# Attention and feed-forward block: subtraction in one pass, new places for transfers and tanh, six banks for the last group's scores

## The reference

```
x = x + attn(wkv(x, fside, fside, w, u, cond), w_qkv, w_o)
x = x + ffn(wkv(x, fside, fside, w2, u2, cond), w_gate, w_up, w_down)

# wkv(r, k, v): k = v = fside
ek = exp(min(k, 30)); ekv = ek * v            # running sums a = a*decay + ek, forward and backward
num = nf + nb - ekv + euk*v;  den = df + db - ek + euk      # euk = exp(min(u + k, 30))
out = sigmoid(r) * num / max(den, 1e-8) * (0.8 + 0.2*tf)

# attn: 16 heads of 32, causal
probs = softmax(mask(q @ k.T / sqrt(32)));  return (probs @ v) @ w_o.T

# ffn: inputs and weights rounded to blocks of 32 with a shared exponent
return q_act(silu(q_act(x) @ q_w(w_gate).T) * (q_act(x) @ q_w(w_up).T)) @ q_w(w_down).T
```

## Time and profile before

| | |
|---|---|
| median of 3 runs | 885.54 us (885.06 to 889.25) |
| profiled execution, its own time | 888.3 us |
| its span, first to last instruction | 886.6 us |
| mean granted TensorE clock | 0.949 of 2.4 GHz |
| TensorE busy | 753.3 us (85%) |
| VectorE busy | 755.0 us (85%) |
| ScalarE busy | 510.0 us (58%) |
| DMA issues `stacks<-rows`, SP and POOL | 128 each, 128 KB each |

### The profile page before, as it was taken

The page is one execution under the profiler, slowest core; times in us unless marked ns, Lnnn a source line. Parts: engine busy times, 40 slices in busy tenths (PEclk is TensorE's granted clock), DMA queues, the critical chain, the costliest instruction groups (busy, mean ns, idle before and its releaser), DMA issues.

```text
span 886.6 us, 10871 instructions
## 1 busy us (share of the span) xinstructions
PE 753.3 (85%) x3980; PEld 393.7 (44%) x4017; DVE 755.0 (85%) x1070; ACT 510.0 (58%) x754; POOL 74.8 (8%) x149
## 2 busy tenths in 40 slices
PE   4667659698789999988799999888999998989785
PEld 1222224345444444455444444454444444557674
DVE  4899999998998878989988798899897888743887
ACT  4966655368575474577763664867736636443440
POOL 1000001102000002111000021110000131200000
PEclk9786678899999999999999999999999999999998
DMA  9623311456100004754010037540100084500001
GB/s 335 253 88 107 106 60 40 98 124 167 48 25 24 1 12 124 191 141 116 13 36 1 13 76 221 155 119 13 36 1 12 13 221 129 125 1 1 1 1 48
DMA packets 31253, 73.08 MB, mean 82 GB/s; under 512 B 5856, under 2 KB 6880, under 8 KB 29408
## 3 DMA queue, kind: packets, MB, share of 16 engines
q1 hardware_dynamic: 19584, 46.67, 17.5%
q0 software_dynamic: 6144, 16.79, 8.1%
q10 hardware_dynamic: 5472, 8.92, 3.2%
HBM read 34.61 MB, written 4.19 MB: 44 GB/s over the span
## 4 chain that ended last, share of the span: by engine, by line
PE 40%; DVE 31%; issue 10%; ACT 8%; DMA 6%; SPq 3%; POOL 1%; ACTq 0%; DVEq 0%
PE bank L1591 9%; DMA stacks<-rows 5%; PE bank L1469 5%; PE bank L1458 4%; PE bank L1373 4%; DVE negmax L1068 4%; SPq L331 3%; PE bank L1440 3%; ACT region L575 3%; PE bank L1496 2%; PE bank L1381 2%; PE bank L1407 2%; DVE num L974 2%; PE bank L1387 2%; DVE fn L960 1%
## 5 line engine op out<-in xcount | busy, mean ns | idle before, releaser
L331 POOL DMA_DIRECT2D stacks<-rows x128 | 70.7, 560 | 696.7 <-DVE region L1114 347.1
L575 ACT ACTIVATE region<-bank 128x384 f32<-128x384 f32 (+1 forms) x192 | 95.5, 522 | 54.5 <-PE bank L1443 52.5
L1440 PE MATMUL bank<-stacks 128*128 128x512 f32 (+3 forms) x256 | 104.7, 415 | 25.0 <-ACT region L575 24.8
L1068 DVE TENSOR_REDUCE negmax<-bank 128x4 f32<-128x512 f32 (+2 forms) x96 | 98.5, 1035 | 27.6 <-PE bank L1414 14.7
L1381 PE MATMUL bank<-h,wqkv 128*128 128x512 f32 x256 | 115.5, 605 | 0.0
L1407 PE MATMUL bank<-stacks 128*128 128x128 f32 (+3 forms) x256 | 77.7, 398 | 12.8 <-DVE negmax L1068 6.6
L1381 PEld LDWEIGHTS bank<-h,wqkv 128*128 128x128 f32 x256 | 49.0, 194 | 58.0 <-issue 57.6
L1440 PEld LDWEIGHTS bank<-stacks 128*128 128x128 f32 x256 | 49.7, 194 | 54.5 <-ACT region L575 45.3
L1442 PE MATMUL bank<-maxrow,pick 128*128 128x384 bf16 (+3 forms) x236 | 72.5, 307 | 0.0
L1373 PE MATMUL bank<-wqkv,h 128*128 128x512 f32 x128 | 61.4, 624 | 4.7 <-DVE h L1008 4.7
L1643 PE MATMUL bank<-region,ident 128*128 128x512 f32 x64 | 49.5, 934 | 12.7 <-DVE identb L919 12.7
(11 more groups left out here) (196 smaller groups left out, 1526.0 us busy)
## 6 DMA issues: line engine op xcount, KB each, us to landing
stacks<-rows SPq DMA_DIRECT2D x128, 128.0 KB, 3.4
stacks<-rows POOLq DMA_DIRECT2D x128, 128.0 KB, 4.6
...
```

The source lines that it names most:

```text
L331: eng.dma_start(stacks[HD * r:HD * r + HD, at:at + 2, i, :].bitcast(F32), rows[mine, q:k + 1:k - q, :]).then_inc(stacked[s][i], 16)
L575: nc.scalar.activation(probs[:, i, P_AT[tiles[0]]:P_AT[tiles[0]] + columns], bank[4 + n % 2][:, 0:columns], ACT.Exp, scale=SCALE).then_inc ...
L1068: nc.vector.tensor_reduce(o, scored, AX_X, ALU.max, negate=True).then_inc(max_taken, 1)
L1440: nc.tensor.matmul(o, ks[s][:, i, P * t:P * t + P], qs[s][:, i, P * t:T], start=True, stop=False, skip_group_check=True)
```

## The change

It has nine parts; no matmul, exponential or scan is added or left out.

1. `less_ident` and the places 2 to 5 of `rows` (under the new name `rounded_rows`, the same memory) are of type fp32r, so that the subtraction has two rounded operands.
2. The next batch's group 0 transfers wait for the second rounding to eighths (`rounded_8`) and no longer for the second scaled quarter (`iq_ready`).
3. SP sends the load of x into `h` only when group 2's transfers have landed. The tanh stands behind `cap_exp(5)`, and its second table load behind `floored(4)`.
4. TensorE: group 1's subtraction of the next batch stands before the last quarter of the down projection. In turns 1 to 3 the projection of group 2 goes before the first scores, and that of the values before slots 4 and 5.
5. ScalarE: `late_high_parts` and both weighings of unit 2 stand before `copy_maxima(0)`.
6. VectorE: `backward(1, 1)` and `add_own(1)` stand before the residual at a turn's end; a new order of the turn's first steps for b > 0.
7. VectorE: a maximum is taken before `backward(4, 1)`, `backward(5, 0)`, `backward(5, 1)` and `forward(6, 0)`.
8. Last group: scores by key go round banks 4, 5, 0, 1, 2, 3; tile n waits for the exponential of tile n - 6, and tile 2 for all maxima.
9. ScalarE in the last group: the maxima's copy and one exponential before the weighings of unit 6; `cap_exp(7)` behind the ninth exponential.

The diff, without the longer lists of part 6 (shown as order below):

```diff
@@ -78,7 +78,7 @@
         identb = sb("identb", [P, P], BF16)
-        less_ident = sb("less_ident", [P, P], F32)
+        less_ident = sb("less_ident", [P, P], F32R)
         hide_kq = sb("hide_kq", [P, P], BF16)
@@ -110,8 +110,9 @@
         v_sb = sb("v_sb", [P, TT, C], F32)
+        rows_at = (nc.sbuf_base + 31) // 32 * 32
         rows = sb("rows", [P, 8, T], F32)
-        halves = rows[:, 2:6, :].bitcast(F32R)
+        rounded_rows = nc.alloc_sbuf_tensor_at("rounded_rows", [P, 4, T], F32R, offset=rows_at + 2 * T * 4)
         attn = [rows[:, n, :] for n in (0, 6, 1, 7)]
@@ -257,6 +258,10 @@
+        def key_bank(g, n):
+            return bank[(4, 5, 0, 1, 2, 3)[n % 6]] if g == GROUPS - 1 else bank[4 + n % 2]
         def qk_banks(g):
@@ -326,10 +331,11 @@
                 mine = slice(HD * i, HD * i + HD)
+                source, base = (rounded_rows.bitcast(F32), 2) if g < 2 else (rows, 0)
                 q_high, q_low, k_high, k_low = ((2, 3, 4, 5), (2, 3, 4, 5), (2, 0, 4, 6), (3, 1, 5, 7))[g]
...
                     eng.dma_start(stacks[HD * r:HD * r + HD, at:at + 2, i, :].bitcast(F32),
-                                  rows[mine, q:k + 1:k - q, :]).then_inc(stacked[s][i], 16)
+                                  source[mine, q - base:k - base + 1:k - q, :]).then_inc(stacked[s][i], 16)
@@ -364,10 +370,12 @@
                     sp.wait_ge(v_ready, b * TT + TT)
+                    for head in stacked[0]:
+                        sp.wait_ge(head, (b + 1) * (STACK_INC * GROUPS // 2))
                     sp.dma_start(h[:, :, :], x[b + 1]).then_inc(h_in, 16)
...
                 if more:
-                    sp.wait_ge(iq_ready, b * FC + 2)
+                    sp.wait_ge(rounded_8, b * FC + 2)
                     stack(sp, b + 1, 0, 0, 2)
@@ -423,7 +431,7 @@
                 if b + 1 < B:
-                    pool.wait_ge(iq_ready, b * FC + 2)
+                    pool.wait_ge(rounded_8, b * FC + 2)
                     stack(pool, b + 1, 0, 2, HG)
@@ -542,7 +550,7 @@
                     act.wait_ge(qk_ready, projected(b, g) + s + 1)
-                    nc.scalar.activation(halves[:, 2 * s, :], qk_bank[s][:, :], ACT.Copy).then_inc(qk_high, 1)
+                    nc.scalar.activation(rounded_rows[:, 2 * s, :], qk_bank[s][:, :], ACT.Copy).then_inc(qk_high, 1)
@@ -555,7 +563,7 @@
                     act.wait_ge(qk_rest, b * 4 + 2 * g + s + 1)
-                    nc.scalar.activation(halves[:, 2 * s + 1, :], qk_bank[s][:, :], ACT.Copy).then_inc(qk_low, 1)
+                    nc.scalar.activation(rounded_rows[:, 2 * s + 1, :], qk_bank[s][:, :], ACT.Copy).then_inc(qk_low, 1)
@@ -573,7 +581,7 @@
                     nc.scalar.activation(probs[:, i, P_AT[tiles[0]]:P_AT[tiles[0]] + columns],
-                                         bank[4 + n % 2][:, 0:columns], ACT.Exp,
+                                         key_bank(g, n)[:, 0:columns], ACT.Exp,
                                          scale=SCALE).then_inc(p_ready, 1)
@@ -624,11 +632,11 @@
                 copy_raw(b, 2)
-                copy_maxima(b, 0)
                 late_high_parts(b)
-                copy_values(b, (0,))
                 weigh(b, 2, 0)
                 weigh(b, 2, 1)
+                copy_maxima(b, 0)
+                copy_values(b, (0,))
@@ -640,13 +648,7 @@
                 weigh(b, 3, 1)
-                if more:
-                    table(0)
-                    act.wait_ge(h_in, b * 16 + 32)
-                    nc.scalar.activation(h[:, :, :], h[:, :, :], ACT.Tanh, scale=0.5).then_inc(tanh_ready, 1)
                 copy_maxima(b, 1)
-                if more:
-                    table(6)
                 cap_exp(b, 4)
@@ -664,9 +666,15 @@
                 cap_exp(b, 5)
+                if more:
+                    table(0)
+                    act.wait_ge(h_in, b * 16 + 32)
+                    nc.scalar.activation(h[:, :, :], h[:, :, :], ACT.Tanh, scale=0.5).then_inc(tanh_ready, 1)
                 copy_maxima(b, 2)
...
                 floored(b, 4)
+                if more:
+                    table(6)
@@ -684,15 +692,16 @@
                 own_exp(b, 6)
+                copy_maxima(b, 3)
+                exps(b, 3, 0, 1)
                 weigh(b, 6, 0)
-                copy_maxima(b, 3)
                 weigh(b, 6, 1)
-                exps(b, 3, 0, 2)
+                exps(b, 3, 1, 2)
                 sum_reciprocal(b, 2)
-                exps(b, 3, 2, 6)
+                exps(b, 3, 2, 9)
                 cap_exp(b, 7)
-                exps(b, 3, 6, 12)
+                exps(b, 3, 9, 12)
                 load_k(b, 6)
@@ -1220,14 +1229,22 @@
...
+                if b:
+                    forward(b, 2, 0)
+                    maxima(b, 0, 0)
+                    maxima(b, 0, 1)
+                    forward(b, 2, 1)
+                    maxima(b, 0, 2)
+                    maxima(b, 0, 3)
+                else:
...
@@ -1261,10 +1278,10 @@
                 maxima(b, 2, 4)
-                backward(b, 4, 1)
                 maxima(b, 2, 5)
...
+                backward(b, 4, 1)
                 add_own(b, 4)
@@ -1272,16 +1289,16 @@
                 finish(b, 4)
+                maxima(b, 3, 2)
                 backward(b, 5, 0)
-                maxima(b, 3, 2)
+                maxima(b, 3, 3)
                 backward(b, 5, 1)
-                maxima(b, 3, 3)
                 add_own(b, 5)
                 maxima(b, 3, 4)
-                forward(b, 6, 0)
                 maxima(b, 3, 5)
...
+                forward(b, 6, 0)
                 forward(b, 6, 1)
@@ -1353,6 +1370,8 @@
                 backward(b, 9, 0)
+                backward(b, 9, 1)
+                add_own(b, 9)
                 for j in range(CJ):
@@ -1384,7 +1403,7 @@
                 pe.wait_ge(qk_high, b * HIGHS + 2 * g + s + 1)
-                nc.tensor.matmul(qk_banks(g)[s][:, :], less_ident[:, :], rows[:, 2 + 2 * s, :],
+                nc.tensor.matmul(qk_banks(g)[s][:, :], less_ident[:, :], rounded_rows[:, 2 * s, :],
                                  start=False, stop=True, skip_group_check=True).then_inc(qk_rest, 1)
@@ -1432,11 +1451,16 @@
                             pe.wait_ge(wq_steps, wq_done[0])
-                if g > 0 or n >= 2:
+                if g == GROUPS - 1 and n == 2:
+                    pe.wait_ge(max_taken, (b + 1) * (GROUPS * SLOTS))
+                if g == GROUPS - 1 and n >= 2:
+                    if n >= 6:
+                        pe.wait_ge(p_ready, b * (GROUPS * UNITS) + g * UNITS + n - 5)
+                elif g > 0 or n >= 2:
                     pe.wait_ge(p_ready, b * (GROUPS * UNITS) + g * UNITS + n - 1)
...
                     c = P_AT[t] - P_AT[tiles[0]]
-                    o = bank[4 + n % 2][:, c:c + CAUSAL[t]]
+                    o = key_bank(g, n)[:, c:c + CAUSAL[t]]
                     nc.tensor.matmul(o, ks[s][:, i, P * t:P * t + P], qs[s][:, i, P * t:T],
@@ -1524,18 +1548,30 @@
...
+                if b:
+                    pe.wait_ge(raw_copied, 2 * b + 1)
+                    project_qk(b, 2, 0)
+                    scores(b, 0, 0)
+                    scores(b, 0, 1)
+                    project_qk(b, 2, 1)
+                    scores(b, 0, 2)
+                    scores(b, 0, 3)
+                    project_values(b, 0, 0, 2)
+                    scores(b, 0, 4)
+                    scores(b, 0, 5)
+                else:
...
@@ -1598,6 +1634,9 @@
                 for n, c in enumerate(ROUNDING):
+                    if n == FC - 1:
+                        for s in range(2):
+                            leave_low(b + 1, 1, s)
                     pe.wait_ge(iq_ready, b * FC + n + 1)
```

40 lines of the change are left out of this document (20 added, 20 removed).

## The result

The changed kernel takes 873.4 us (median of 4 runs, 870.7 to 874.2) against 885.3 of the kernel before; the ratio is 0.985 (95% interval 0.983 to 0.987). On a second chip it was 872.0 in 5 runs against 887.3, ratio 0.983 (0.981 to 0.985).

What follows compares the result with a forecast made beforehand. No engine bounds everywhere: TensorE does from attention's end through the feed-forward part; the rest passes between engines. Gains of 5.5, 3.9, 3.9 and 2.9 sum to 16.2: 888.3 becomes 872.1, less 2.8 to the median, forecast 869, range 862 to 880.

Steps and rivals of the forecast that it cites:

- Subtractions in one pass: TensorE ahead of the feed-forward part: one pass instead of two saves 0.6 us in each of turns 0 to 2.
- Transfers after the eighths: Turn's end: next group 0 transfers issue 6 us earlier, landing near 529; subtractions cost 0.7, save idle 0.98 and 1.4.
- Start of turns 1 to 3: New orders there, with the second transfer's landing deciding: turns 1 and 2 lose 0.2 us each, turn 3 gains 0.8.
- The first rival: Second transfer still lands at 551.4 to 552; turns 1 to 3 each lose 1.4 to 2 more; 874 us, chance 0.18.
- the late high parts are set by the landing: Start of a turn: ScalarE's late high parts wait for the second transfer to land, at most 15.8 behind turn 2's subtraction.
- L: Landing time of the second transfer at turn 2's start: forecast 550, bounds 548.5 (stores cost nothing) and 552.2.
- Start of turn 0: High parts and weighings move into ScalarE's wait for the maxima: 2.3 us, and 0.7 at VectorE's next group wait: 3.0.
- x behind the stacks: Between groups 0 and 1: x issued after group 2's stacks land; gains 1.6 us in turns 1 and 2.
- keeps exactly that: VectorE gains its 1.61 us wait between groups 0 and 1 and, not waiting again in groups 1 and 2, keeps it.
- the 2.19 goes: TensorE's 2.19 us wait for group 2's stacks vanishes, as POOL's eight land some 7 us behind their first issue.
- Maxima earlier and six banks: Groups 1 to 3: TensorE and ScalarE run about 2.9 ahead; gain 1.9 us in turns 0 to 2, 2.1 in turn 3.
- The clock falls: Rival: waits at a turn's start put group 0 at the low clock, some 9 us per turn; 896 us, chance 0.04.

Runs made afterwards that it cites:

- the whole old start: Changed kernel with transfers' wait, TensorE, VectorE and ScalarE orders at the start of turns 1 to 3 as before the change; 868.6 us, ratio 0.979.
- stores: Changed kernel with SP sending the four result stores and the load of xt only after the second transfer's landing; 864.2 us, ratio 0.975 to the kernel before.
- weighings: Changed kernel with both weighings of unit 2 ahead of the late high parts in turns 1 to 3; 867.8 us, ratio 0.978 to the kernel before.

## Why the prediction was right, and where it was not

The forecast of 869 was 3 to 4 low. Its sum of 16.2 is within 1 of what both spans fell by (15.3, 16.4). What is left comes from the step to the medians: the profiled execution before was 2.8 above its median, that of after is at its own. The 2.8 rested on a median of three runs; on the four chips of the experiments the kernel before has medians of 886.5 to 888.5. But the sum hides errors that cancel.

- *Subtractions in one pass* (0.6 in turns 0 to 2): the mis-sized term. Undone it costs 9.2. I had counted only the pair ahead of the feed-forward part; there it measured 0.4, and a call got 0.53 cheaper (1.88 and 0.82 for a pair), not 0.84. The pair at a turn's start, too, I had at nothing: the whole old start has there the same orders as the kernel before and the single pass, and its stage is 0.5, 0.7 and 1.6 shorter (34.22, 33.97 and 33.97 against 34.67, 34.66 and 35.61, one trace each). The pair in the last quarter of the down projection, which I took as a cost of 0.7, would have cost 1.9 with two passes, and turn 0's first scores would be late: with one pass VectorE's wait of 0.92 for them is gone. That explains 4 to 5 of the 9.2; the rest stays open.
- *Transfers after the eighths*: the high parts start without a wait at 518.57, or 528.6 in the clock of before, where I had 529. Its worth was rightly put at nothing by itself: with the whole old start the landing is 29.7 to 30.5 behind the start of the down projection, with the early transfers 30.0 to 30.8.
- *Start of turns 1 to 3* (-0.2, -0.2, +0.8): the stages read -0.3, -0.1 and +0.5, and the landing came at 550.5 in the clock of before (540.48 + 10.0), where I had 550. So the numbers hold, though in part by luck: they contain the single pass's share just named, which the new order gave away again. The judgement on it didn't hold: the step put the weighings and then the maxima's copy between landing and first exponential into its sum and never asked what the stage would be without them. Against the whole old start the package loses 3.4 (2.3 to 2.9 in its three stages). What sets this stage in the changed kernel is the landing (stores: 7.8 in the whole time, 5.8 in the stages) and what ScalarE does behind it (weighings: 4.2).
- *The first rival, that the landing doesn't move*: it held in turn 2. My 551.4 was no landing but the time at which ScalarE came to the late high parts, with no idle before them. SP's last two issues of turn 2 in the kernel before:

```profile
L331 SPq DMA_DIRECT2D stacks<-rows x2: 1214/1348/1481, 543.5 to 545.0; - x2
DMA to landing us min/median/max: 5.5/6.0/6.6
```

The last landed 5.5 behind 545.0, at 550.5, as the changed kernel's did in that clock. Counted from the start of the down projection, the landings were at 31.0, 30.1 and 31.9 before and at 30.0 to 30.8 in both traces after: 0.6 to 0.8 earlier in turn 1, nothing in turn 2, 1.2 to 1.8 in turn 3. So "the late high parts are set by the landing" was true of turn 3 and not of turn 2, where the maxima came last. With the stores behind it the landing comes 2.2 earlier; my bound for stores that cost nothing was 1.5 below L, short of that, and its 2.8 for the stores has no row. The Trainium skill (DMA: Bandwidth & Descriptors, "Issuing engines are not separate DMA queues") says that transfers issued by different engines run on the same sixteen DMA engines and interleave. The trace agrees: with SP's transfers and, until 535.7, POOL's under way these were busy for 0.98 of the time from 528 to 540.
- *Start of turn 0* (3.0): 3.2 up to the first exponential and 1.5 in group 0. Part of the excess is the wait of 0.92, and VectorE's 0.69 for group 1's second maximum, which I had not listed, goes too.
- *x behind the stacks* (1.6 in turns 1 and 2): 4.5 when undone, 4.8 with turn 0's share. That VectorE "keeps exactly that" did not hold: where both traces have as many falls of the clock, in turns 0 and 1, a turn keeps 1.0 to 1.1. The step "the 2.19 goes" held in the second trace and not in turn 2 of the first, where POOL's eight landed 8.45 behind their first issue and not 7.
- *Maxima earlier and six banks* (1.9, and 2.1 in turn 3): the mechanism is right, the cap was wrong. I said that VectorE is ahead by 1.6 only and keeps 1.9. Undoing the banks costs 2.2 a turn in full (9.3 in all), undoing the maxima 2.2 in turns 1 and 2 and nothing in turn 3 (7.2 in all); the two losses are the same gain, which needs both parts. So the chain through TensorE and ScalarE sets groups 2 and 3, and VectorE's two waits are its mark. The waits of 0.76 and 1.16 went, except behind a fall of the clock.
- *The clock falls*: the rival was a whole group at the low level, 9 per turn, and that did not come. But two of the three starts of turns 1 to 3 have a fall in either trace after, and none has one before. A fall costs 1.6 there (15.87 from the first exponential of group 0 to its values, against 14.29). Turn 3's +1.4 is a fall and a wait of 0.39 in one trace, a wait of 0.78 for the stacks in the other. With five falls where the trace of before had two, up to 3 x 1.6 = 5 were given back; one trace of before is too few to call that shown. The granted clocks of all runs speak for a smaller loss: their mean is 0.949 in 42 runs of the kernel before and 0.945 in 9 of the changed one, which makes some 3 us of lost clock more (an estimate: 0.055 of 872 less 0.051 of 887). The price I gave was also half of what it should be: if 18.9 us of work run at half the clock they lose 18.9, not 9. A small version of this rival, some falls more per run, belonged into the sum, and the mark I gave ("a granted clock below 1 there") was met by a forecast that held.
